# A two-layer transformer on one core: scale factors before the first steps, last values behind the heads' values, and the field behind the third rotation

## What is computed

```python
x = x + attn0(softmax((x + stage_embed) @ fside.T) @ fside)
x = x + fp4_ffn(x @ W[category] + b[category])
x = x + attn1(zX * lap_x(x) + zY * lap_y(x) + zR * x * (1 - x))
x = x + moe(cond2(x))
```

```python
scale = max(max(abs(xb)) / 6, 1e-12)
q = grid[nearest(abs(xb / scale))] * sign(xb) * scale
```

## Time and profile before

| | |
|---|---|
| median of 3 runs | 2429.3 us (2426.37 to 2429.45) |
| the profiled execution's own time | 2426.79 us |
| its span | 2424.7 us |
| granted clock of TensorE, mean | 0.975 |
| first layer in its steady state | about 141 to 690 |
| joint of the layers | about 690 to 870 |
| second layer in its steady state | about 870 to 1470 |
| third stage | from about 1470 on |

### The profile page before, as it was taken

How to read it: one execution, slowest core, us unless ns; L and a number is a source line. 1 busy time by engine, 2 the same in 40 slices (tenths; PEclk the granted TensorE clock), 3 DMA queues, 4 the chain that set the end, 5 groups by cost and what they waited for, 6 DMA issues and landing times.

```text
span 2424.7 us, 53715 instructions
## 1 busy us (share of the span) xinstructions
PE 2248.6 (93%) x18240; PEld 2041.3 (84%) x18240; DVE 1852.2 (76%) x5119; ACT 1292.3 (53%) x3839; POOL 1019.9 (42%) x1078
## 2 busy tenths in 40 slices
PE   3799999999976899999999999899999999999999
PEld 2688878888865778888888887899999999999999
DVE  5878888888878666666666765578878888888876
ACT  1667666666662455655555554433336555555522
POOL 5535454454525455455555553033332222222073
PEclk8999999999997899999999999999999999999999
DMA  4523333333330322222222222222126777777443
GB/s 138 182 85 107 103 95 116 91 113 95 99 110 3 99 57 58 72 60 58 70 64 57 66 57 75 64 36 43 39 94 213 233 235 237 233 232 239 142 120 124
DMA packets 203301, 267.36 MB, mean 110 GB/s; under 512 B 61670, under 2 KB 171510, under 8 KB 192278
## 3 DMA queue, kind: packets, MB, share of 16 engines
q1 hardware_dynamic: 194166, 245.27, 33.4%
q0 software_dynamic: 8864, 18.66, 2.9%
HBM read 175.84 MB, written 43.94 MB: 91 GB/s over the span
## 4 chain that ended last, share of the span: by engine, by line
PE 58%; DVE 19%; POOL 8%; issue 7%; ACT 6%; DMA 1%; SPq 0%; POOLq 0%; DVEq 0%; ACTq 0%
PE bank L55 48%; PE bank L136 6%; POOL P L1796 2%; DVE xe L928 2%; PE bank L1322 2%; DVE Ph L821 2%; DVE tb L1654 1%; DVE qm L917 1%; DVE xe L933 1%; DVE sgs L955 1%; ACT P L1495 1%; PE bank L1362 1%; ACT Ph L657 1%; DVE rot0s L881 1%; DVE hb L965 1%
## 5 line engine op out<-in xcount | busy, mean ns | idle before, releaser
L1495 ACT ACTIVATE P<-P,mx 128x144 f32<-128x144 f32 x512 | 206.2, 405 | 229.2 <-DVE mx L1616 228.2
L2642 POOL DMA_INDIRECT xE<-d_y,ixs x78 | 112.1, 1437 | 336.2 <-PE bank L136 300.7
L55 PE MATMUL bank<-xD_hi,w1e_lo 128*128 128x256 f32 x880 | 251.1, 285 | 0.0
L55 PE MATMUL bank<-w2e_hi,hrD_hi 128*128 128x256 f32 x880 | 249.0, 283 | 0.0
L55 PE MATMUL bank<-w2e_lo,hrD_hi 128*128 128x256 f32 x880 | 248.9, 283 | 0.0
L55 PE MATMUL bank<-w2e_hi,hrD_lo 128*128 128x256 f32 x880 | 248.9, 283 | 0.0
L55 PE MATMUL bank<-xD_lo,w1e_hi 128*128 128x256 f32 x880 | 245.9, 279 | 0.0
L55 PE MATMUL bank<-xD_hi,w1e_hi 128*128 128x256 f32 x880 | 245.6, 279 | 0.0
L1127 POOL TENSOR_TENSOR xe<-xe 128x704 f32<-128x704 f32 (+3 forms) x64 | 88.0, 1375 | 353.9 <-DVE xe L936 353.7
L1796 POOL TENSOR_TENSOR P<-P,rs 128x512 f32<-128x512 f32 x128 | 133.1, 1040 | 246.0 <-DVE rs L1625 243.5
L2251 ACT ACTIVATE hD<-bank,b1E 128x256 f32<-128x256 f32 x312 | 127.0, 473 | 197.2 <-PE bank L55 182.8
(11 more groups left out here) (324 smaller groups left out, 7959.7 us busy)
## 6 DMA issues: line engine op xcount, KB each, us to landing
w1raw<-in_ew SPq DMA_DIRECT2D x39, 1024.0 KB, 5.9
w2raw<-in_ew SPq DMA_DIRECT2D x39, 1024.0 KB, 4.9
stack<-d_rot SPq DMA_DIRECT2D x256, 96.0 KB, 2.7
K<-Kn SPq DMA_DIRECT2D x256, 72.0 KB, 2.0
d_rot<-QKh SPq DMA_DIRECT2D x64, 256.0 KB, 3.1
Q<-Qn SPq DMA_DIRECT2D x256, 64.0 KB, 2.0
d_ys<-oE SPq DMA_DIRECT2D x39, 256.0 KB, 2.6
d_rot<-QKl SPq DMA_DIRECT2D x32, 256.0 KB, 3.1
```

The source lines that it names most:

```text
L55: inst = e.matmul(out, l, r, start=k == 0, stop=k == len(pairs) - 1)
L1495: inst = e.activation(P1[t % 2][:, n, :], P1[t % 2][:, n, :], ACT.Exp, bias=mx1[t % 2][:, 2 * g + sg:2 * g + sg + 1], scale=-1.0, accum_ou ...
L2642: e.indirect_dma_start(out=xE[q % 2][c], out_offset=None, in_=d_y, in_offset=bass.IndirectOffsetOnAxis(ap=ixs[r % 4][:, c:c + 1].bitcast(U ...
```

## The change

Three functions are edited, and nothing is computed otherwise; only the order changes.

In the first layer, `hidden_scales` of the second half moves from p=0 to p=7 of the turn before, between the second product L965 and the parts 1 and 2 of the first half's steps. `invert_sums(b)` moves from the end of p=7 to a place behind the first half's scales. On TensorE `first_values(b+1)` at p=0 moves behind `turn_sums(b-1)`, and both behind the values of the head pair; ACT takes its two copies in the same new order.

In the second layer, the field moves from the end of s=1 to s=2, between the maxima and the copy of the turned probabilities. The rotation n=2 moves from s=2 to the end of s=1, where the field stood, and the rotation n=3 from behind the maxima of s=2 to before them.

```diff
@@ pe_ab
                     scores(P + 1)
-                    if p == 0:
-                        first_values(b + 1)
-                        turn_sums(b - 1)
                     if p % 2 == 0:
                         values(P // 2 - 1)
+                    if p == 0:
+                        turn_sums(b - 1)
+                        first_values(b + 1)
@@ act_ab
                         first_copy(b + 1)
+                        sums_copy(b - 1)
                         x1_high(b + 1)
-                        sums_copy(b - 1)
@@ dve_ab
                     if p == 0:
-                        hidden_scales(b - 2, 1)
                         x1_low(b + 1)
                         hidden_steps(b - 2, 1)
...
                     if p == 7:
                         hidden_scales(b - 1, 0)
+                        invert_sums(b)
                         gated(b - 1, 1, 0)
                         gated(b - 1, 1, 1)
                         multiply(b - 1, 1, 0)
                         hidden_steps(b - 1, 0, (0,))
                         multiply(b - 1, 1, 1)
+                        hidden_scales(b - 1, 1)
                         hidden_steps(b - 1, 0, (1, 2))
-                        invert_sums(b)
@@ dve_c
                     if s == 2:
-                        rotate(b + 1, 2)
+                        rotate(b + 1, 3)
...
                     if s == 2:
-                        rotate(b + 1, 3)
+                        field(entering(b))
+                        field_sum(entering(b))
                     if s == 5:
                         rotate(b + 1, 6)
                     copy_turned(t)
+                    if s == 1:
+                        rotate(b + 1, 2)
...
-                    if s == 1:
-                        field(entering(b))
-                        field_sum(entering(b))
```

## The result

The changed kernel took 2432.34 us (median of 20 runs, 2430.03 to 2437.75), the kernel before 2429.46 on the same occasions (20 runs, 2425.57 to 2432.62). The ratio is 1.0016, with a 95% interval of 1.0009 to 1.0022: 2.9 slower by the medians. I had forecast 2428.5, that is no change with a lean to faster. The time lies in the range and within 0.2%, but clear of no change, and on the other side.

What follows compares the result with a forecast made beforehand. TensorE was taken as nearly full (93%), so VectorE edits count only where TensorE waits. Terms +11.8+0.9+0+4.0+0.7-17.0 = +0.4 gave 2427.2 or 2429.7 by profile or median; the middle is 2428.5, range 2408 to 2440.

Steps and rivals of the forecast that it cites:

- First layer, +11.8: First layer, 13 samples: L928, L933 and L936 now wait for three GpSimd passes, L936 ending 0.91 later each time.
- The ends of the range, -1.67 and +1.68: First layer, per sample: -1.67 if nothing collides, +1.68 if GpSimd keeps the port pair through its three passes.
- L928 misses its turn: First layer rival: GpSimd's second pass comes before L928, +1.33 a sample, 2434; chance 0.15 together with GpSimd keeping the pair.
- afresh: First layer rival: a blocked step starts only after the pass, at full length, 0.43 more a sample, 2434; chance 0.05.
- VectorE keeps its turn: First layer rival: L936 follows L933 at once, ahead of GpSimd's third pass, -0.23 a sample, 2414; chance 0.18.
- no collision: First layer rival: no collision worth the name, -1.67 in each of 13 samples, 2395; chance 0.10.
- TensorE then waits for the scores until 315.5 in any case, so nothing more: First layer, TensorE: the quantised half's turn waits for GpSimd until some 314.1, at no further cost.
- Joint, +0.9 + 0 + 4.0 + 0.7 = 5.6: Last samples and joint: boundary near 683 +0.9, near 731 0, drain near 776 +4.0, block near 825 +0.7.
- The 4.0 for the field: Drain near 776: the field stands behind the third rotation, delaying squares and TensorE's norm sum from 791.62 to some 795.4.
- the "0" of the block near 731: Boundary near 731: the first half is later, the second equal, so no cost.
- Second layer, -17.0: Second layer: the field goes behind the third rotation, TensorE no longer waits for L1654, 1.31 less in each of 13 samples.

Runs made afterwards that it cites:

- shortened passes: Changed kernel with GpSimd's add and subtract over 32 of 704 columns only, result not the reference's: 2390.76 us in one run, 38.9 below the kernel before.
- split scales: Kernel before with second layer's order changed from b >= 1, L832 earlier, L914 before the maxima, L917 and L919 between their groups: 2417.05 against 2441.33, ratio 0.9898.
- the first layer's part alone: Kernel before with only the edits in `pe_ab`, `act_ab` and `dve_ab`, `dve_c` as before: 2461.60 against 2443.85 us, ratio 1.0083.
- the joint in old order: Changed kernel with the field behind the third rotation only from b >= 1, the joint of the layers as before: 2442.51 against 2441.33 us, ratio 1.0003.
- VectorE's edits alone: Changed kernel with TensorE's and ACT's order as before, `dve_ab` and `dve_c` as changed: 2445.57 against 2443.85 us, ratio 1.0010.
- nearly all steps ahead of GpSimd: Kernel before with second layer's order from b >= 1, most second-half steps before GpSimd's first pass, first half's turn at p=2: 2475.17 against 2429.65, ratio 1.0190.
- the second layer's part alone: Kernel before with only the edits in `dve_c`: 2432.87 against 2443.85 us, ratio 0.9953.
- late form: Kernel before with the second layer's edits only from b >= 1: 2412.65 against 2429.65, ratio 0.9920; again 2424.39 against 2441.33, ratio 0.9925.
- extra turn: Changed kernel in which TensorE at p=1 turns the heads' probabilities twice into the same banks: 2429.77 against 2429.65 us, ratio 1.0003.

## Why the prediction was wrong

By its own terms, each against the traces:

- **First layer, +11.8.** The twelve periods between copies L695 are longer by 15.8, of which 4.3 is the next point's; that leaves 11.5. The forecast for twelve of the thirteen changes was 10.9; the 13th lies in the joint. Right, and by the mechanism foretold: L928, L933 and L936 each wait for one pass. The ends of the range, -1.67 and +1.68, were both far off, and so were the rivals "L928 misses its turn" (+1.33), "afresh", "VectorE keeps its turn" and "no collision". The shortened passes and the split scales show the same rule at other places.
- **"TensorE then waits for the scores until 315.5 in any case, so nothing more".** This is the step that failed. I found rightly that the turn of the quantised half would wait for GpSimd until some 314.1 (320.37 less 6.27 is 314.10), and rightly that this adds nothing to the chain. But I counted the path only, and no term of the sum was for the clock. Behind an idle stretch of 1.40 and one of 0.62 the granted clock fell in three of twelve samples: 1.05 + 2.22 + 1.05, **+4.3** in the trace. The three kernels that have TensorE's new order with the wait of 1.4 (the changed one, the first layer's part alone, the joint in old order) show slow stretches in three, three and five of twelve periods. The seven traces with TensorE's first layer as before show none, whether its wait is 0.76 (VectorE's edits alone) or absent. The new order with shortened passes, where the wait is gone, shows none either. With the wait at 0.8 by extra work there are two. The kernel with nearly all steps ahead of GpSimd waits 3.40 at another place and has them in seven, at 1.6 each. So the long waits go with the falls; what decides in which sample the clock falls stays open.
- **Joint, +0.9 + 0 + 4.0 + 0.7 = 5.6.** With the 13th change of the first layer, which lies in the same stretch, the forecast is 6.5; measured +7.8 in the trace. By an estimate the clock explains more than the difference: the 11 us more at the lower level, at 0.31 to 0.34 each, are 3.4 to 3.7. What is left, 4.1 to 4.4, is below the forecast, not above it. The 4.0 for the field has 3.5 in the pair with equal clocks. The squares do hold TensorE's norm sum as foretold: it waits 5.1 for L1537 in the changed kernel. TensorE's wait for VectorE's L949 ends 122.1 after the last L695 before, and 124.9 to 125.8 with the first layer's edits: +2.8 to +3.7, where I had 1.8 with the 13th change. But TensorE had run 6 to 11 us longer at the lower level by then, so the runs do not show that the "0" of the block near 731 was too small.
- **Second layer, -17.0.** 12 x -1.34 from the fourth to the last L1537, and a period of 1.1 ahead of them: -17.1. Right.
- **The filling of the pipeline.** Its end lies between 140.8 and 143.7 in the traces. The kernel before, the second layer's part alone and its late form are the same program up to there, and have 140.8, 143.1 and 141.4. So the 2.9 that the changed kernel's trace has more need not be the change's. My expectations after the result had put it down to TensorE's order; that isn't shown.

In the traces, then: 2.9 (filling) + 11.5 + 4.3 + 7.8 - 17.1 - 1.7 (from the last L1537 to the end) = 7.7, the distance of the spans (2432.3 and 2424.7) within a rounding. My sum had +0.4. Of what it lacked, 4.3 is the clock in the steady first layer, 0.6 the collisions, and 1.3 the joint, which the clock may explain by the estimate above. The rest is filling and end, which differ between executions by about as much anyway.

By the medians 2.5 were missing, and no trace of one execution can divide them. Two things of many executions agree with the clock. The first layer's terms (11.8 + 0.9 + 0 + 0.7 = 13.4) are too low, as its part alone costs 17.8, by its interval 17.1 at least; the second layer's (-17.0 + 4.0 = -13.0) lie within the interval of its part alone. And the mean granted clock is lower than beside it in every kernel with the first layer's new order on VectorE: medians of 0.9675 against 0.971 (joint in old order, 12 executions and 17), 0.968 against 0.970 (VectorE's edits alone), 0.9715 against 0.974 (extra turn), 0.966 against 0.974 (nearly all steps ahead of GpSimd), and by a hair 0.969 against 0.970 (first layer's part alone) and 0.973 against 0.974 in the one run with shortened passes. With the second layer's part, whole or late, or with the split scales, it is not lower.

The chances were not far off (0.38 for within 0.2%), but the number leant the wrong way, since every term that I left at nothing could only cost.

## What to carry over

A stall that one engine suffers behind another is not removed by letting the first go ahead if that delays the other's passes: count which instructions of the same kind now meet them. Where two engines take turns, look for the gaps between the passes and have the short steps waiting there; that gave 0.4 a sample here, and needed no change of what is computed. And a wait of TensorE that was off the path was not free here: put a price on the clock too, from rows at both levels. And before a difference between two single traces is given to an edit, compare the granted clock of the stretch.

## What was not expected of the hardware

- In the steady first layer the granted clock fell to 1.2 GHz for 3.4 us, once for 6.8, behind idle stretches of 1.40 and 0.62, in some samples and not in others of the same timing, each time at a price of 0.8 to 2.2. In two executions of the same program it also stood low for 48 and 55 us of the joint.
- The kernel before took 12 to 14 longer on two occasions than on the third (2443.85 and 2441.33, against 2429.65). Only differences measured beside each other could be used. The traces put this in the third stage, which no edit touches: from the last L1537 to the end they have 1003.0 to 1010.1 on the third occasion and 1014.2 to 1026.5 on the two others, while kernels with the same order have the same periods to 0.05 on all of them. Why is open.
- Saving 0.26 on VectorE's chain in each sample (L832) changed nothing, because a turn tied to GpSimd's passes lay behind it.
